# Order of the work at the entry to the expert tiles of an attention and mixture-of-experts kernel

## The reference

```python
x = x + _L0_xattn_ref(_layernorm(x), ctx, ctx, Wh, wg_w, wo_w, gn_gamma, gn_beta)
x = x + _L0_ffn_ref(_layernorm(x), Wg, W1, W3, W2, Ws1, Ws3, Ws2)
# _L0_ffn_ref, with xt the 2048 x 512 tokens, INTER = 352, E = 16, TOPK = 4:
h = silu(einsum('td,eid->eti', xt, W1)) * einsum('td,eid->eti', xt, W3)
y = einsum('etd,te->td', einsum('eti,edi->etd', h, W2), combine)   # 4 experts of a token have weight
z = silu(xt @ Ws1.T) * (xt @ Ws3.T) @ Ws2.T                        # both shared halves
return y + z
```

## Time and profile before

| quantity | value |
|---|---|
| median of 3 runs | 955.37 us |
| lowest and highest run | 953.28 and 955.61 us |
| the profiled execution's own time | 954.32 us |
| its span, first to last instruction | 952.7 us |
| PE busy | 914.0 us, 96% of the span |
| VectorE, GpSimd, ScalarE busy | 557.2, 494.8, 332.3 us |
| mean granted TensorE clock | 0.989 |

### The profile page before, as it was taken

How to read it: one execution, slowest core, us unless ns; L and a number is a source line. 1 busy time by engine, 2 the same in 40 slices (tenths; PEclk the granted TensorE clock), 3 DMA queues, 4 the chain that set the end, 5 groups by cost and what they waited for, 6 DMA issues and landing times.

```text
span 952.7 us, 19359 instructions
## 1 busy us (share of the span) xinstructions
PE 914.0 (96%) x4962; PEld 811.7 (85%) x4963; DVE 557.2 (58%) x1103; ACT 332.3 (35%) x708; POOL 494.8 (52%) x346
## 2 busy tenths in 40 slices
PE   8999998899999996899999999999999999997998
PEld 5778876688889985899999999999999999896997
DVE  6656766898885542344444444444444444465997
ACT  4466553443334221233333333333333333321221
POOL 1137777772276675044644665456666634046771
PEclk9999999999999999899999999999999999998999
DMA  6739995664677767657785777777778755577884
GB/s 210 259 116 388 390 402 183 238 201 139 194 268 243 249 221 229 203 154 247 218 260 165 248 247 248 245 246 231 248 247 255 246 166 154 155 212 209 265 264 131
DMA packets 180649, 218.97 MB, mean 230 GB/s; under 512 B 56576, under 2 KB 124160, under 8 KB 180224
## 3 DMA queue, kind: packets, MB, share of 16 engines
q1 hardware_dynamic: 118080, 123.49, 40.4%
q0 software_dynamic: 20816, 79.44, 24.9%
q10 hardware_dynamic: 41712, 15.54, 6.0%
HBM read 127.38 MB, written 91.03 MB: 229 GB/s over the span
## 4 chain that ended last, share of the span: by engine, by line
PE 75%; DVE 9%; issue 5%; DMA 5%; ACT 3%; SPq 1%; POOL 1%; ACTq 0%; DVEq 0%; POOLq 0%
PE ps L1153 14%; PE ps L1154 14%; PE ps L1155 14%; PE ps L1205 8%; PE ps L1207 8%; PE ps L1206 8%; DMA hblk<-h_d 2%; PE ps L1008 2%; PE ps L1021 2%; DVE st L1450 1%; PE ps L955 1%; DVE res L1448 1%; SPq L408 1%; DMA xslot_d<-scat,sloti 1%; DVE st L1267 1%
## 5 line engine op out<-in xcount | busy, mean ns | idle before, releaser
L1153 PE MATMUL ps<-whi,xhi 128*128 (+1 forms) x888 | 291.3, 328 | 10.7 <-issue 8.6
L1154 PE MATMUL ps<-wlo,xhi 128*128 (+1 forms) x888 | 288.7, 325 | 0.0
L1155 PE MATMUL ps<-whi,xlo 128*128 (+1 forms) x888 | 288.6, 325 | 0.0
L1153 PEld LDWEIGHTS ps<-whi,xhi 128*128 128x128 f32 x888 | 169.3, 191 | 17.4 <-issue 12.7
L1525 DVE TENSOR_TENSOR hrow<-ps,sg 128x352 f32<-128x352 f32 x95 | 49.8, 524 | 224.6 <-ACT sg L827 224.4
L1154 PEld LDWEIGHTS ps<-wlo,xhi 128*128 128x128 f32 x888 | 169.5, 191 | 4.0
L1155 PEld LDWEIGHTS ps<-whi,xlo 128*128 128x128 f32 x888 | 169.0, 190 | 0.0
L827 ACT ACTIVATE sg<-ps 128x352 f32<-128x352 f32 x111 | 51.5, 464 | 283.9 <-PE ps L1155 283.9
L834 ACT ACTIVATE xhi<-ps 128x512 fp32r<-128x512 f32 x112 | 66.9, 597 | 150.7 <-DVE ps L1486 150.6
L560 POOL TENSOR_TENSOR wlo<-raw,whi 128x2816 fp32r<-128x2816 f32 x16 | 100.5, 6283 | 2.4 <-POOL whi L558 0.3
L654 POOL DMA_INDIRECT raw<-yslot_d,sloti x64 | 69.3, 1083 | 57.7 <-DMA yslot_d<-ysb 28.3
(11 more groups left out here) (199 smaller groups left out, 1597.7 us busy)
## 6 DMA issues: line engine op xcount, KB each, us to landing
raw<-wexp_in POOLq DMA_DIRECT2D x18, 2176.0 KB, 11.4
xslot_d<-zero SPq DMA_DIRECT2D x10, 2048.0 KB, 21.2
xg<-xslot_d SPq DMA_DIRECT2D x320, 64.0 KB, 2.1
yslot_d<-ysb SPq DMA_DIRECT2D x80, 256.0 KB, 2.2
h_d<-hrow ACTq DMA_DIRECT2D x79, 192.0 KB, 2.5
hblk<-h_d SPq DMA_DIRECT2D x79, 192.0 KB, 2.6
xg<-xn_d SPq DMA_DIRECT2D x128, 64.0 KB, 3.4
xq<-x_in SPq DMA_DIRECT2D x16, 256.0 KB, 3.4
```

Of the source, the lines that this page charges most:

```text
L1153: pe.matmul(ps[:, 2 + m, 0:INTER], xh, wh, start=(k == 0), stop=False)
L1154: pe.matmul(ps[:, 2 + m, 0:INTER], xh, wl, start=False, stop=False)
L1155: mm = pe.matmul(ps[:, 2 + m, 0:INTER], xl, wh, start=False, stop=(k == KT - 1))
```

## The change

- **First expert rows ahead.** DVE computes the `hrow` of e0 before it adds the last `down` of the shared half to the residual, not after it.
- **Odd gate halves in bank 7.** In the expert run the gate half of odd tiles goes to bank 7. `up` of tile t then waits only for the silu of tile t - 2 before its gate half, and for `h_ready` of tile t - 1 before its value half, for every expert tile.
- **Scatter two products closer.** Scatter t waits for `up` of tile t - 1 instead of tile t + 1.
- **Weight sets serial.** The load of set o + 1 is issued inside `split(o)`, when set o has landed and set o - 1 is split; so the load of set 4 waits for set 3 to land.
- **One unused tile moved behind.** The comparison is with 63, 65, ..., 75. With 72 or 73 used tiles that makes 2 unused tiles in front where it made 3; the total stays 80.
- **The stores the gather waits for.** A second entry of the table counts the odd used tiles, for two more small DVE instructions.

```diff
+NTAB = NRP + E + 1 + NL + 1
+        def gate_bank(base, p):
+            return 7 if base == NT and p else 2
...
                 hold(pool, raw_loaded[p], 16 * (half + 1))
+                if type(o) is not int or 2 < o < NW - 1:
+                    next_raw(o + 1, 1 - p)
                 hold(pool, mm1, 2 + before)
...
             def next_raw(o, p):
-                hold(pool, w13_ready, o + 1)
-                hold(pool, w2_ready, o + 1)
-                pool.dma_start(raw[:, p, :]..., wexp[bass.ds(o + 2, 1), ...]...)
+                hold(pool, w13_ready, o - 1)
+                hold(pool, w2_ready, o - 1)
+                pool.dma_start(raw[:, p, :]..., wexp[bass.ds(o, 1), ...]...)
...
-                pool.wait_ge(mm1, 2 + (min(t + 2, NT) if t else 1))
+                pool.wait_ge(mm1, 2 + max(t, 1))
...
-            def set_and_next(o, p, half):
-                split(o + 2, p, half + 1, tiles_through(o + 2))
-                if type(o) is int and o == 0:
-                    pool.wait_ge(first_lo, 2 * NT)
-                    load_weights(1, 3)
-                next_raw(o + 2, p)
-            pipeline(pool, NW - 4, [(0, set_and_next)])
-            for o in range(NW - 2, NW):
-                split(o, o % 2, o // 2, tiles_through(o))
+            def set_on(t, p, half):
+                split(t + 3, 1 - p, half + 1 + p, tiles_through(t + 3))
+            split(2, 0, 1, tiles_through(2))
+            pool.wait_ge(first_lo, 2 * NT)
+            load_weights(1, 3)
+            pipeline(pool, NW - 4, [(0, set_on)])
+            split(NW - 1, (NW - 1) % 2, (NW - 1) // 2, tiles_through(NW - 1))
...
-            stored = pool.value_load(order[0:1, NRP + E:NRP + E + 1], ...)
-            for p in range(2):
+            for p, at in enumerate((NRP + E, NTAB - 1)):
+                stored = pool.value_load(order[0:1, at:at + 1], ...)
                 hold(pool, y_stored[p], stored)
...
-                    act.activation(sg[:, :], ps[:, 2, 0:INTER], ACT.Silu).then_inc(silu, 1)
+                    act.activation(sg[:, :], ps[:, gate_bank(base, p), 0:INTER], ACT.Silu).then_inc(silu, 1)
...
-                    two = base == NT and type(t) is int and t in (2, 3)
                     pe.wait_ge(x_lo, base + t + 1)
-                    if 1 in halves and not two:
+                    if base == NT:
+                        pe.wait_ge(silu, base + t - 1 if type(t) is not int or t else base)
+                    elif 1 in halves:
                         pe.wait_ge(h_ready, base + t)
...
-                        if two and m:
+                        if base == NT and m:
                             pe.wait_ge(h_ready, base + t)
+                        bank = 3 if m else gate_bank(base, p)
...
-                ... const[:, C_TILE + NT * TOPK + 1:C_TILE + NT * TOPK + 2 * NL:2], total[:, 0, 0:1], None, ALU.is_ge))
+                ... const[:, C_TILE + NT * TOPK - 1:C_TILE + NT * TOPK - 2 + 2 * NL:2], total[:, 0, 0:1], None, ALU.is_ge))
...
+                step(dve.tensor_scalar(ecmp[:, 0:NR // 2, 0], const[0:1, C_TILE + 1:C_TILE + NR:2], ntile[0:1, 0, E - 1:E], 16.0, ALU.is_lt, ALU.mult))
+                step(dve.tensor_reduce(tabf[:, NRP + E + 1 + NL:NTAB], ecmp[:, 0:NR // 2, 0], AX, ALU.add))
...
+            def first_row(t, r, turn):
+                if type(t) is int and t == NT - 1:
+                    h_row(NT)(0, 0, 0)
+            def later_rows(t, r, turn):
+                if type(t) is not int or t >= 1:
+                    h_row(NT)(t, r, turn)
-            ... (0, route_2), (-1, add_shared(0)), (0, h_low_on), ...
+            ... (0, route_2), (-1, first_row), (-1, add_shared(0)), (0, h_low_on), ...
-            stream(dve, [(NR, True, [(0, h_row(NT)), ...
+            stream(dve, [(NR, True, [(0, later_rows), ...
```

More of the change, by code:

```diff
@@ L250, in xattn_moe @@
         sloti = sb3("sloti", [P, NT * TOPK], I32)
-        tabf = sb3("tabf", [1, NRP + E + 1 + NL], F32)
-        order = sb3("order", [1, NRP + E + 1 + NL], I32)
+        tabf = sb3("tabf", [1, NTAB], F32)
+        order = sb3("order", [1, NTAB], I32)
         packf = sb3("packf", [1, NR // XG], F32)
@@ L566, in next_raw @@
             def next_raw(o, p):
-                hold(pool, w13_ready, o + 1)
-                hold(pool, w2_ready, o + 1)
-                pool.dma_start(raw[:, p, :].rearrange("p (c n) -> p c n", c=PIECES), wexp[bass.ds(o + 2, 1), :, :, :].rearrange("a c p n -> p (a c) n")).then_inc(raw_loaded[p], 16)
+                hold(pool, w13_ready, o - 1)
+                hold(pool, w2_ready, o - 1)
+                pool.dma_start(raw[:, p, :].rearrange("p (c n) -> p c n", c=PIECES), wexp[bass.ds(o, 1), :, :, :].rearrange("a c p n -> p (a c) n")).then_inc(raw_loaded[p], 16)
             def affine(t, p, half):
@@ L629, in tiles_through @@
                 return pool.value_load(order[0:1, bass.ds(o + NRP - 2, 1)], min_val=NT, max_val=NT + NR)
-            def set_and_next(o, p, half):
-                split(o + 2, p, half + 1, tiles_through(o + 2))
-                if type(o) is int and o == 0:
-                    pool.wait_ge(first_lo, 2 * NT)
-                    load_weights(1, 3)
-                next_raw(o + 2, p)
-            pipeline(pool, NW - 4, [(0, set_and_next)])
-            for o in range(NW - 2, NW):
-                split(o, o % 2, o // 2, tiles_through(o))
+            def set_on(t, p, half):
[5 more added lines that the diff above has]
+            split(NW - 1, (NW - 1) % 2, (NW - 1) // 2, tiles_through(NW - 1))
             pool.wait_ge(w2_ready, NW)
-            stored = pool.value_load(order[0:1, NRP + E:NRP + E + 1], min_val=8 * NT * TOPK, max_val=16 * (NR // 2))
-            for p in range(2):
+            for p, at in enumerate((NRP + E, NTAB - 1)):
+                stored = pool.value_load(order[0:1, at:at + 1], min_val=8 * NT * TOPK, max_val=16 * (NR // 2))
                 hold(pool, y_stored[p], stored)
@@ L1152, in fn @@
                             wh, wl = whi[:, a, c:c + INTER], wlo[:, a, c:c + INTER]
-                            pe.matmul(ps[:, 2 + m, 0:INTER], xh, wh, start=(k == 0), stop=False)
-                            pe.matmul(ps[:, 2 + m, 0:INTER], xh, wl, start=False, stop=False)
-                            mm = pe.matmul(ps[:, 2 + m, 0:INTER], xl, wh, start=False, stop=(k == KT - 1))
+                            pe.matmul(ps[:, bank, 0:INTER], xh, wh, start=(k == 0), stop=False)
+                            pe.matmul(ps[:, bank, 0:INTER], xh, wl, start=False, stop=False)
+                            mm = pe.matmul(ps[:, bank, 0:INTER], xl, wh, start=False, stop=(k == KT - 1))
                     if 1 in halves:
@@ L1612, in r_places @@
                 step(dve.tensor_reduce(total[:, 0, 0:1], ntile[:, 0, :], AX, ALU.add))
-                step(dve.tensor_scalar(total[:, 1, 0:NL], const[:, C_TILE + NT * TOPK + 1:C_TILE + NT * TOPK + 2 * NL:2], total[:, 0, 0:1], None, ALU.is_ge))
+                step(dve.tensor_scalar(total[:, 1, 0:NL], const[:, C_TILE + NT * TOPK - 1:C_TILE + NT * TOPK - 2 + 2 * NL:2], total[:, 0, 0:1], None, ALU.is_ge))
                 step(dve.tensor_reduce(total[:, 0, 1:2], total[:, 1, 0:NL], AX, ALU.add))
@@ L1783, in combine @@
                 return fn
-            pipeline(dve, NT, [(2, x_turn_on), (1, x_low_on), (0, h_mult_on), (0, route_1), (0, route_2), (-1, add_shared(0)), (0, h_low_on),
+            def first_row(t, r, turn):
[4 more added lines that the diff above has]
+                    h_row(NT)(t, r, turn)
+            pipeline(dve, NT, [(2, x_turn_on), (1, x_low_on), (0, h_mult_on), (0, route_1), (0, route_2), (-1, first_row), (-1, add_shared(0)), (0, h_low_on),
                                (0, second_set), (0, expert_rows)], ramp=11, ring=XG)
-            stream(dve, [(NR, True, [(0, h_row(NT)), (-2, turn_first), (-2, low_first), (2, x_turn_r), (-2, turn_later), (2, x_low_r), (-2, low_later),
+            stream(dve, [(NR, True, [(0, later_rows), (-2, turn_first), (-2, low_first), (2, x_turn_r), (-2, turn_later), (2, x_low_r), (-2, low_later),
                                      (0, None), (0, None), (0, None)], None),
```

## The result

The changed kernel takes 929.4 us as the median of 4 runs (928.63 to 930.60), the kernel before in the same measurement 954.33 (951.97 to 955.61). The ratio is 0.9743, with a 95% interval of 0.9717 to 0.9768. Forecast were 931.5 us, with a range of 928 to 941, counted from a median of 955.37 before. The profiled execution took 928.63 us, with a span of 927.1.

A forecast was written before the change was run, and what follows sets the result against it. PE bounds the kernel, busy 914.0 of 952.7 us, losing 17.95 at the expert entry and 9.28 in the second shared half. Gains 14.95 + 9.28 less 0.53 make 23.7 us: 931.5 us forecast, range 928 to 941.

The forecast's parts named there:

- part 1: Expert entry: last scatter issued at 341.50, 11.3 us earlier, landing 5.14 us later, so SP goes on at 346.7.
- Rival D: Entry: scatter does not come sooner because its landing grows with denser issues; entry 2.65 us worse, 949 us; chance 0.03.
- part 2: Entry: e2 now waits for the scatter but is covered; `load_h` of e0 issued at 357.3, `down` of e0 covered.
- part 3: Entry: rows ahead and bank 7 remove waits between `up`s; no term of their own, no gain in the undisturbed run.
- rival E: Expert run: the second wait in each `up` makes PE's stream stumble; 963 us at 0.4 us per tile; chance 0.02.
- part 4: Entry: set 3's load catches `load_h` of e1, `down` of e1 starts at 371.9; 3.0 us lost, bounds 0 and 9.
- rival A: Entry: set 4's load catches `load_h` of e2, costing 7.5 us, some 9 with half clock; 938 to 941 us; chance 0.15.
- The rule of turns: Entry: DMA engines alternate queues by packet, read as half and half; the 3.0 us loss would be 0; prediction rejected it.
- Rival B: Entry: the `hblk` loads escape the weight loads, so no loss there; 928.7 us; chance 0.08.
- part 5: Second shared half: gather begins 11.84 us earlier, so VectorE doesn't wait and 9.28 us come back; lower bound near 5.
- Rival C: Second shared half: the earlier gather brings nothing, the 9.28 us stay lost; 941 us; chance 0.06.
- part 6: First shared half: two more small VectorE instructions delay a `down` that waits for VectorE, costing 0.53 us; bound 0.

The follow-up runs named there:

- e0: Not a run: the first expert tile; the middle stretch starts at its `up`, 345.90 us into the kernel before and 346.54 into the changed one.
- two experiments: Changed kernel with bank 7 and its waits undone, 933.47 us; changed kernel with bank 7 kept, `h_ready` wait back ahead of gate halves in PE's loop, 934.33 us.
- a third: Kernel before with only bank 7 and its split waits added: 943.13 us, against 949.91 us for the kernel before in the same set.
- e76: Not a run: a late expert tile; the middle stretch ends at its `down`, taking 487.41 us in the kernel before and 470.43 in the changed one.
- three other profiles: Changed kernel with the scatter two products later, 938.55 us; with the `h_ready` wait put back, 934.33 us; with late set 4 load and no second entry, 923.0 us.

## Why the prediction was right

The total was right to 2.1 us, and the mechanism of its two large terms holds. It came out that close partly because two errors cancel, and 1.0 us of the 2.1 is the base: the kernel before measured 954.33 here and not 955.37.

- **Scatter (part 1): right.** Last issue 342.12, forecast 341.5. It landed in 2.7 us and not in 5.14, so SP went on at 344.89, forecast 346.7. Undone, the middle stretch loses 11.7 us. Rival D is out.
- **One tile behind, SP's queue (part 2): right.** `load_h` of e0 is issued at 356.19, forecast 357.3 (SP began 1.8 us sooner and took 11.3 us instead of 10.6), and nothing waits for the tokens of e2. The price of the cover showed when it was taken away: 6.19 us idle at `up` of e2 in the kernel with the late scatter.
- **Bank 7 (part 3): the step that failed**, twice. "Bank 7 gains nothing there" looked at one place without a loop edge. The gaps at the 17 edges were 4.7 us; two experiments bring them back, larger (6.6 and 6.9 us), and a third removes them alone. "Alone they would save nothing" was wrong as well: bank 7 alone gave 6.8 us between the medians, of which the loop's 4.7 are shown. The profile has 5.3 more at the entry, but there the scatter landed sooner, and their cause stays open. The extra wait before the value half costs nothing readable, so rival E is out.
- **The weight loads (part 4): the mechanism right, the place and size off.** The loads came at 358.39 and 370.58, forecast 357.6 and 369. `load_h` of e1, issued at 360.20, was caught, and `down` of e1 started at 371.54, forecast 371.9. But the loss does not end there. The store of e2's row landed with set 3, so SP came to `load_h` of e3 only at 374.40, within the load of set 4. This is rival A, one tile later (its 938 to 941 counts the 3.0 of part 4 twice; by the bound of 9 the sum gives 937.7): `load_h` of e2, at 370.70, was issued while GpSimd still issued the load of set 4 (370.58 and 0.92 long) and was not waited for, much as argued against A; that of e3 was caught. `down` of e3 started at 386.10 instead of 384.3, and half clock behind it took 1.7 more. So the term is 17.95 - 4.15 - 1.66 = 12.1 instead of 14.95. The experiment with the late load of set 4 shows the cause: without that load in the way the middle stretch is 5.0 us shorter. What the change calls serial has no part in the gain.
- **The rule of turns: the trace agrees, the prediction's use of it was wrong.** DMA: Bandwidth & Descriptors of the Trainium skill, section Queues, rings and completion order, has a DMA engine go round its queue rows by packets. The packets of the trace do so, 66, 66 and 67 of the three queues from 366 to 367 us. "Half and half" took the turns for shares of bytes. In packets a store is as long as the weight load, 528 each, and `load_h` of e3 has 512 packets of token loads ahead of it in its queue. Not part of the rule is the late first packet, after more than 3.5 us instead of 1.15. The two make 9.14 and 9.38 us for 192 KB. Rival B is out.
- **Gather (part 5): right in this profile, with little margin.** 9.28 forecast, 9.26 measured, with 11.68 us of earlier start against the tiles, forecast 11.84. The kernel with three unused tiles in front gives back 5.7 of it. It keeps the second entry of the table, and its gather begins 2.61 us ahead of `down` of e76, where it was 2.62 behind before (835.93 and 833.31): so the entry accounts for the other 3.6, though no run leaves out the entry with 75 places filled. In three other profiles about 2 us of the 9.26 are lost again to a `combine` that waits. Rival C is out.
- **Two small instructions (part 6): right**, the idle time in front of `down` grows from 0.93 to 1.47 us.

The terms as measured: 13.80 at the entry, less 1.66 of half clock, 4.7 at loop edges, 9.26 at the end, less 0.53, which makes 25.6; the profiled executions differ by 954.32 - 928.63 = 25.7. Against the forecast of 23.7, 4.7 were missing and 2.8 too much.

**What stays open.** Why a short transfer issued beside a weight load has its first packet only 3 to 4 us later is not shown. That larger packets for the short transfers would get them through sooner follows from the turns, but no run tried it. Why the gap at the loop edge is 0.28 us in the kernel before and 0.4 in the two experiments is open too. Why the loop edge shows when PE waits for `h_ready` ahead of the gate half was not measured inside PE's sequencer. An explanation that fits, argued only: the row of the tile before is done 1.05 us after its `up` ends (360.35 to 361.40), so a wait ahead of the gate half lets the sequencer run only about 1 us ahead of the matmuls, and one 12 matmuls later lets it run 1.9 us further.

## What to carry to other kernels

A gap that comes once in a pass of a loop doesn't show in any one place that is looked at, so measure the distance over many passes before a wait is called free. Where a long load and a chain of short round trips meet, ask for each store and load of the chain what is in flight when it is issued, and put the long load behind the chain: one load issued 11 us later brought 5 us here. Compare the two in packets and not in bytes, and count what stands ahead in the same queue. A wait is judged by how far ahead of its instructions' turn it is released, so move it to the last instruction that needs it even when the engine shows no idle time.

## What the runs showed of the hardware

- A 192 KB transfer that is issued 3 to 4 us after a 2,176 KB weight load lands with it: 9.14 us for a store and 9.38 for a load, where 2.7 and 2.5 us are usual. The queues take turns packet by packet, whatever the size: 66, 66 and 67 packets in one microsecond, of 4.2 KB in the weight load and 0.37 KB in the store; in the kernel before 77, 75 and 77 from 379 to 380 us. A store issued 3.1 us behind the weight load had its first packet 3.8 us after its issue, one with none in flight after 1.15. Issued 0.28 us ahead of the weight load, as in the kernel with bank 7 alone, such a load was not waited for.
- PE has 0.28 us more between two matmuls at the turn of its loop (0.4 in the two experiments), when a wait released late stands ahead of the last 24 matmuls of the pass, and none when it stands ahead of the last 12.
- After 2.09 us of idle PE its clock stood at the lower level for a whole `down`, 0.43 instead of 0.23 us between matmuls. After the 1.38 us ahead of `down` of e1 it did not fall: the granted clock is 1.00 from 352 to 385 us. The length of the idle time alone doesn't decide it: after 2.37 us with bank 7 undone and 2.83 us with three unused tiles in front the clock stayed at the higher level too. The first of the two, in the timeline of PE and in the stretch behind it:

```profile
387.25 0.50 PE L1210 MATMUL ps<-whi,hhi_odd 128*128 x1 [2.37 <-DVE hlo_odd L1507]
```

```profile
387.00:394.00 7.00, 6.75 (x37) 6.24 (x38) 2.83 (x6) 2.05 (x4) 6.83 (x2) 1.00 0.70 202
```
